# Second cross attention of a Perceiver-like kernel: maxima in two pieces, softmax by PSUM bank, and output products alternating with turned banks

## The chip, the cores and the metric

One core of one Trainium2 chip. The metric is the device time of one execution in microseconds (us), given as the median of several runs. TensorE does matrix products and transposes, VectorE and ScalarE elementwise work and reductions, GpSimd issues the gathers here, and SyncE issues the weight loads. All five run their own instruction streams and wait for each other by semaphores. PSUM, into which TensorE writes, has 8 banks of 512 fp32 columns; SBUF holds the rest.

## The reference, cut to what matters

Two layers, each of cross attention, self attention and a feed-forward part, on x of shape (2, 128, 512) with a context of (2, 2048, 512). The change is in the second layer's cross attention alone:

```python
def _L1_xattn_ref(q, kv, Wq, Wkv, Wc):            # q: layernorm(x), kv: the context
    qp = jnp.einsum('bld,ed->ble', q, Wq)
    scores = jnp.einsum('bld,bmd->blm', qp, kv)   # 128 x 2048 for each batch
    idx = jnp.argmax(scores, axis=-1)
    mem = jnp.take_along_axis(kv, idx[..., None], axis=1)   # 128 chosen rows
    mk, mv = jnp.split(jnp.einsum('bld,ed->ble', mem, Wkv), 2, axis=-1)   # 32 wide each
    qh = qp.reshape(b, l, 16, 32).transpose(0, 2, 1, 3)
    logits = jnp.einsum('bhld,bmd->bhlm', qh, mk) / sqrt(32)
    attn = softmax(logits)                        # 16 heads, 128 x 128 each
    out = jnp.einsum('bhlm,bmd->bhld', attn, mv)  # then heads side by side
    return jnp.einsum('bld,ed->ble', out, Wc)     # added to x
```

## The kernel before

Each part of the model is one function per engine (`..._pe`, `..._act`, `..._dve` for TensorE, ScalarE and VectorE), and the order in each function is written by hand; no scheduler changes it. The parts follow one another on every engine: first cross attention, mixer, experts, then `cross1_*` (the part in question), `linear_*` and the feed-forward part. A part starts with a norm of x_res: statistics on VectorE, a square root on ScalarE, and eight transposes on TensorE. While TensorE waits, `keep_clock(pe, bank, n)` lets it do n products of no use (an identity by constants, 256 columns) into a spare bank. A fp32 product is two records in the trace, a transpose one.

Weights come as 151 blocks of 1 MB through a ring of four, issued by SyncE; a block's slot is loaded again when `blk_used` says that it was read. The stage uses two of them (`BLK_X1` for the queries, `BLK_X1 + 1` for the output). The context comes back into SBUF by GpSimd's queue (`ctx_back`), during the last expert and the start of the stage.

The stage before, with the batches b = 0 and 1:

1. TensorE: queries `qpT` (L1817), copied by ScalarE (L1886). Then the scores of batch 0 in banks 4 to 7 and of batch 1 in banks 0 to 3, 16 products of 512 columns each (L1827).
2. VectorE, for each batch: the eight largest of 2048 columns (L1907), their index (L1909), and the row's number `pick` (L1911). GpSimd gathers the chosen rows by an indirect DMA into `mem` (L2306).
3. TensorE turns `mem` (L1836) for each batch, with 16 fillers between the two; ScalarE copies it to `memT` (L1889). Keys of both batches in one go (L1840), then values of both (L1844).
4. VectorE spreads the keys by heads into `mkz` (L1914), ScalarE copies the values (L1891). TensorE makes the logits of one batch in four banks (L1853), four heads a bank.
5. VectorE: maximum over each head (L1919) and subtraction (L1920) of a whole batch, 128 x 2048. ScalarE: the exponential of the whole batch (L1894). VectorE: sum (L1923), reciprocal (L1924) and scaling (L1925) of the whole batch. TensorE has 15 fillers meanwhile.
6. TensorE turns the 16 heads of a batch (L1862), ScalarE copies each bank (L1897), TensorE mixes the values with weights of 32 columns (L1867), ScalarE copies the result (L1900), and TensorE makes the output product in banks 2 and 3 (L1875), all for batch 0 and then batch 1.
7. VectorE adds both batches' output to x_res in one operation (L1927), from which the next norm starts.

Of the kernel before, what the change touches and what calls it, by code (L numbers as in the profile page):

```python
# [16 lines left out]
P = 128  # L17
# [98 lines left out]
def build(nc, x, ctxT, ctx_rows, wq, wk, wv, wo, stream, small, cols, rows, consts, out):  # L116
# [6 lines left out]
    with ExitStack() as ctx:  # L123
# [3 lines left out]
        def sem(name):  # L127
            return ctx.enter_context(nc.semaphore(name))
# [153 lines left out]
        NORM_WAIT = {1: (12, 2), 2: (7, 3), 3: (7, 2), 4: (7, 5)}  # L282
# [1500 lines left out]
        top8 = [sb(f"top8_{b}", [P, 8]) for b in range(B)]  # L1783
        at8 = [sb(f"at8_{b}", [P, 8], u32) for b in range(B)]
        pick = [sb(f"pick{b}", [P, 1], u32) for b in range(B)]
        lm = sb("lm", [P, B, H])
        ls = sb("ls", [P, B, H])

        ctx_back = [sem(f"ctx_back{b}") for b in range(B)]
        qp_filled = sem("qp_filled")  # L1790
# [8 lines left out]
        mk_filled = sem("mk_filled")  # L1799
        mkz_ready = sem("mkz_ready")  # L1800
        mv_filled = sem("mv_filled")
        mv_ready = sem("mv_ready")
        la_filled = sem("la_filled")
        la_shift = sem("la_shift")
# [5 lines left out]
        x1o_ready = sem("x1o_ready")  # L1810

        def cross1_pe(pe):
            norm_pe(pe, 3)
            need(pe, BLK_X1)
            for ec in range(C):
# [4 lines left out]
                if ec % 2:  # L1820
                    last.then_inc(qp_filled if ec == 1 else blk_used, 1)
            pe.wait_ge(qp_ready, 2)
            for b in range(B):
                pe.wait_ge(ctx_back[b], KB * 16)
                for kb in range(KB):
                    for c in range(C):
                        last = nc.tensor.matmul(psum[:, 4 - 4 * b + kb, :], qpT[:, c, b * P:(b + 1) * P],  # L1827
                                                ctxT_sb[b][kb][:, c, :], start=c == 0, stop=c == C - 1)
                last.then_inc(pick_scores, 1)
            pe.wait_ge(at_found, 1)  # L1830
            for b in range(B):
                if b:
                    keep_clock(pe, 7, 16)
                pe.wait_ge(mem_arrived[b], 16)
                for c in range(C):
                    last = nc.tensor.transpose(psum[:, 4 + b, c * P:(c + 1) * P], mem[:, b, c * P:(c + 1) * P], C_("ident"))  # L1836
                last.then_inc(memT_filled, 1)
            pe.wait_ge(memT_ready, 2)
            for c in range(C):
                last = nc.tensor.matmul(psum[:, 6, 0:T], S_("x1_k")[:, c, :], memT[:, c, :], start=c == 0, stop=c == C - 1)  # L1840
            last.then_inc(mk_filled, 1)
            for b in range(B):
                for c in range(C):
                    last = nc.tensor.matmul(psum[:, 7, b * DK:(b + 1) * DK], memT[:, c, b * P:(b + 1) * P],  # L1844
                                            S_("x1_v")[:, c, :], start=c == 0, stop=c == C - 1)
            last.then_inc(mv_filled, 1)
            pe.wait_ge(at_found, 2)
            for b in range(B):
                pe.wait_ge(mkz_ready, b + 1)
                if b == 1:  # L1850
                    pe.wait_ge(mv_ready, 1)
                for j in range(C):
                    last = nc.tensor.matmul(psum[:, 4 * b + j, :], qpT[:, j, b * P:(b + 1) * P], mkz[:, b, :, :],  # L1853
                                            start=True, stop=True)
                last.then_inc(la_filled, 1)
            pe.wait_ge(la_shift, 1)
            keep_clock(pe, 3, 15)
            for b in range(B):
                pe.wait_ge(la_ready, b + 1)
                for j in range(C):  # L1860
                    for i in range(4):
                        last = nc.tensor.transpose(psum[:, 4 * b + j, i * P:(i + 1) * P], la[:, b, 4 * j + i, :], C_("ident"))  # L1862
                    last.then_inc(laT_filled, 1)
            for b in range(B):
# [543 lines left out]
```

## Time and profile before

| | us |
|---|---|
| median of 3 runs | 1406.88 |
| the 3 runs | 1405.14, 1406.88, 1409.73 |
| the profiled execution | 1404.22 |
| its span, first to last instruction | 1402.4 |
| mean granted TensorE clock | 0.974 of full |

In the chain that ended last each piece is an engine at work, or "issue" where nothing shown held it back. In the timeline a row is a merged run of instructions with its start, its length and the idle time before it in brackets. The windows view gives for each stretch the busy time of each engine and the clock that TensorE was granted (1.00 is 2.4 GHz, 0.50 is 1.2 GHz; a number between is a mean over both).

### The profile page before, as it was taken

Reading aid. Unit: us, or ns where it says so; the run is one execution under the profiler, and the core shown is the slowest. Engines: PE = TensorE matmul, PEld = TensorE weight load, DVE = VectorE, ACT = ScalarE, POOL = GpSimd, SP = SyncE. Lnnn points to the kernel's source line nnn. Section 1 sums busy time; section 2 is a strip of 40 time slices with the busy share of each in tenths; the row PEclk is TensorE's granted clock in tenths of the full one; section 3 lists DMA queues with packets and bytes.
Section 4 is the critical chain, followed back from the end, with each engine's and each line's share of the span. In section 5 each row is a group of like instructions: output and inputs, shape, how many; then the busy total and the mean of one; then the engine's idle time right before and its main releaser. Section 6 shows DMA issues by size and latency. Waiting matters only on the chain.

```text
span 1402.4 us, 23487 instructions
## 1 busy us (share of the span) xinstructions
PE 1329.9 (95%) x9866; PEld 1136.3 (81%) x9866; DVE 904.0 (64%) x1131; ACT 679.1 (48%) x754; POOL 12.0 (1%) x18
## 2 busy tenths in 40 slices
PE   7999999999999999896899999999898889999998
PEld 6899999889999986665577777777655669999997
DVE  4665666766566656697778888888425667444443
ACT  4534444544444442652377777777303144555442
POOL 0000000000000000000000000000100000000000
PEclk9999999999999999895899999999999999999999
DMA  8111011401010030120089899999920315455552
GB/s 284 35 31 35 20 42 50 124 20 35 20 35 20 20 121 21 71 80 13 30 318 343 344 341 336 341 344 357 348 90 0 120 64 189 172 183 188 186 185 79
DMA packets 50219, 197.66 MB, mean 141 GB/s; under 512 B 12112, under 2 KB 20560, under 8 KB 30416
## 3 DMA queue, kind: packets, MB, share of 16 engines
q1 hardware_dynamic: 47792, 187.41, 36.8%
q0 software_dynamic: 2336, 8.91, 1.8%
q8 instruction: 72, 1.18, 0.3%
q14 instruction: 19, 0.16, 0.0%
HBM read 195.78 MB, written 0.52 MB: 140 GB/s over the span
## 4 chain that ended last, share of the span: by engine, by line
PE 85%; DVE 10%; issue 2%; ACT 1%; DMA 1%; SPq 0%; POOL 0%; POOLq 0%; DVEq 0%; ACTq 0%
PE psum L453 13%; PE psum L2128 13%; PE psum L428 13%; PE psum L1538 8%; PE psum L480 5%; PE psum L1558 4%; PE psum L1541 4%; PE psum L505 4%; PE psum L2110 3%; PE psum L1561 2%; PE psum L2141 2%; PE psum L1570 1%; PE psum L1958 1%; PE psum L464 1%; PE psum L1827 1%
## 5 line engine op out<-in xcount | busy, mean ns | idle before, releaser
L1599 DVE TENSOR_TENSOR arena_r<-ring,arena_r 128x2048 fp32r<-128x2048 f32 x96 | 219.7, 2290 | 35.7 <-ACT arena_r L1593 35.4
L453 PE MATMUL psum<-ring_r,arena_r 128*128 128x256 f32 x1536 | 201.4, 290 | 3.5 <-ACT arena_r L723 2.5
L453 PEld LDWEIGHTS psum<-ring_r,arena_r 128*128 128x128 f32 x1536 | 192.1, 194 | 4.2 <-issue 2.7
L428 PE MATMUL psum<-arena_r 128*128 128x512 f32 x768 | 186.0, 398 | 9.3 <-ACT arena_r L757 9.2
L1593 ACT CAST arena_r<-ring 128x2048 fp32r<-128x2048 f32 x96 | 183.5, 1913 | 16.5 <-PE psum L1541 10.8
L2128 PE MATMUL psum<-arena_r 128*128 128x256 f32 x1536 | 184.5, 283 | 1.1 <-DVE arena_r L2187 1.1
L2128 PEld LDWEIGHTS psum<-arena_r 128*128 128x128 f32 x1536 | 184.4, 192 | 1.2 <-issue 1.2
L428 PEld LDWEIGHTS psum<-arena_r 128*128 128x128 f32 x768 | 143.1, 190 | 41.6 <-issue 8.4
L2081 DVE TENSOR_TENSOR arena_r<-ring,arena_r 128x2048 fp32r<-128x2048 f32 x44 | 100.9, 2292 | 117.0 <-ACT arena_r L2076 117.0
L2076 ACT CAST arena_r<-ring 128x2048 fp32r<-128x2048 f32 x44 | 83.8, 1904 | 111.4 <-PE psum L2128 85.2
L1538 PE MATMUL psum<-arena_r 128*128 128x512 f32 x512 | 132.5, 401 | 1.3 <-issue 1.3
L1538 PEld LDWEIGHTS psum<-arena_r 128*128 128x128 f32 x512 | 94.2, 188 | 23.2 <-issue 5.0
L744 ACT COPY arena<-psum 128x1024 f32<-128x1024 f32 x64 | 61.7, 1016 | 89.6 <-PE psum L480 89.6
L616 DVE TENSOR_TENSOR arena<-arena,psum 128x1024 f32<-128x1024 f32 x64 | 75.2, 1216 | 28.0 <-PE psum L494 28.0
L301 DVE TENSOR_TENSOR arena_r<-arena,arena_r 128x768 fp32r<-128x768 f32 (+2 forms) x25 | 33.8, 1354 | 74.4 <-ACT arena_r L715 56.2
L736 ACT COPY ring<-psum 128x512 f32<-128x512 f32 x64 | 37.2, 582 | 87.1 <-PE psum L453 87.1
L751 ACT ACTIVATE arena<-arena 128x1024 f32<-128x1024 f32 x64 | 66.2, 1058 | 19.8 <-DVE arena L616 18.5
L596 DVE TENSOR_TENSOR arena<-arena 128x512 f32<-128x512 f32 (+1 forms) x128 | 71.5, 559 | 4.4
L1541 PE MATMUL psum<-arena_r 128*128 128x512 f32 x256 | 68.7, 390 | 0.0
L480 PEld LDWEIGHTS psum<-qT,arena 64*128 64x128 f32 x1024 | 59.7, 188 | 9.9 <-issue 9.1
L480 PE MATMUL psum<-qT,arena 64*128 64x128 f32 x1024 | 65.8, 278 | 0.8 <-issue 0.8
L1558 PE MATMUL psum<-arena_r 128*128 128x512 f32 x256 | 64.2, 393 | 0.0
(309 smaller groups left out, 1692.5 us busy)
## 6 DMA issues: line engine op xcount, KB each, us to landing
ring<-in_stream SPq DMA_DIRECT2D x151, 1024.0 KB, 4.9
arena<-in_ctxT POOLq DMA_DIRECT2D x8, 1024.0 KB, 12.3
arena<-in_ctxT SPq DMA_DIRECT2D x7, 1024.0 KB, 7.9
arena<-in_wk SPq DMA_DIRECT2D x16, 256.0 KB, 3.3
wv_in<-in_wv SPq DMA_DIRECT2D x8, 512.0 KB, 3.4
arena<-in_wq SPq DMA_DIRECT2D x16, 256.0 KB, 2.5
arena<-in_wk SPq DMA_DIRECT2D x16, 128.0 KB, 3.2
arena<-in_wo SPq DMA_DIRECT2D x2, 1024.0 KB, 6.3
```

The lines of the kernel that those rows point to most:

```text
L428: last = nc.tensor.matmul(bank, wk_sb[wp][:, c, w], cx[xp][kb][:, c, :], start=c == wp == xp == 0, stop=c == C - 1 and xp == 1)
L453: last = nc.tensor.matmul(bank[:, q * T:(q + 1) * T], cx[xp][kc // 4][:, c, kc % 4 * P:(kc % 4 + 1) * P], wv_sb[wp][:, c, :], start=c == w ...
L480: last = nc.tensor.matmul(psum[:, 2 * half + kc // 4, kc % 4 * P:kc % 4 * P + P], kT[j % 2][a:a + 64, k0:k0 + P], qT[a:a + 64, j % 2, half ...
L616: nc.vector.tensor_tensor(part, part, per_row(psum[:, SPREAD_BANK, 0:P], KC // 2), ALU.subtract).then_inc(shifted, 1)
L1538: nc.tensor.matmul(out, xg[xp][:, c, e, :], hi[:, c, :], start=c == xp == 0, stop=False)
L1541: last = nc.tensor.matmul(out, xg[0][:, c, e, :], lo[:, c, :], start=False, stop=c == C - 1)
L1558: nc.tensor.matmul(psum[:, 5, :], hT[u][hp][:, f, :], hi[:, f, :], start=u == f == hp == 0, stop=False)
L1593: nc.scalar.copy(mwhi[p % MB], ring[k % RING][:, :]).then_inc(moe_hi, 1)
L1599: nc.vector.tensor_tensor(mwlo[p % MB], ring[(BLK_MOE + p) % RING][:, :], mwhi[p % MB].bitcast(fp32), ALU.subtract).then_inc(moe_lo if p < ...
L2076: nc.scalar.copy(whi[j % 2], ring[k % RING][:, :]).then_inc(w_hi, 1)
L2081: nc.vector.tensor_tensor(wlo[j % 2], ring[(BLK_W12 + j) % RING][:, :], whi[j % 2].bitcast(fp32), ALU.subtract).then_inc(w_lo, 1)
L2128: last = nc.tensor.matmul(psum[:, 4 + s, 0:T], w[wp][:, c, :], src[xp][:, c, :], start=c == wp == xp == 0, stop=c == FC - 1 and wp == 1)
```

## The change

Steps 2 to 7 are done by batch and by bank:

- The maximum of the scores is taken in two pieces, over the first 1536 and the last 512 columns, and a third small maximum joins them (`top16`).
- The turning of batch 0's rows and its keys and values stand between batch 1's score products, and batch 0's logits right behind them. The keys and values are made for one batch at a time. 7 fillers stand ahead of batch 1's rows; the 16 and the 15 of before are gone.
- Each bank of logits has its own maximum on VectorE, which is negated and scaled into `nlm`. ScalarE takes the exponential of each head from PSUM with `nlm` as bias, and gives the sum of the head as its accumulator output (`ls`). Subtraction and sum on VectorE are gone; reciprocal and scaling stay, by bank.
- The copies of batch 0's turned banks and of its mixed output move from ScalarE to VectorE; those of batch 1 stay on ScalarE, a bank at a time.
- The values are mixed by bank, 128 columns a product instead of 512. The output product of batch 0 is made in quarters between the turned banks of batch 1; batch 1's quarters follow as their copies arrive.
- x_res is added to in two halves, the first when batch 0's output is complete.
- The fillers of the norm behind the stage write bank 3 instead of 5.

The core of the diff, TensorE first:

```diff
+            def pick_part(b, parts):
+                for n in parts:
+                    kb, c = n // C, n % C
+                    last = nc.tensor.matmul(psum[:, PICK_BANK[b] + kb, :], qpT[:, c, b * P:(b + 1) * P],
+                                            ctxT_sb[b][kb][:, c, :], start=c == 0, stop=c == C - 1)
...
+            def turn_la(b, j):
+                pe.wait_ge(la_ready, C * b + j + 1)
+                for i in range(4):
+                    last = nc.tensor.transpose(psum[:, PICK_BANK[b] + j, i * P:(i + 1) * P], la[:, b, 4 * j + i, :], C_("ident"))
+                last.then_inc(laT_filled, 1)
+
+            def mix_mem(b, j, out):
+                pe.wait_ge(laT_ready, C * b + j + 1)
+                for i in range(4):
+                    last = nc.tensor.matmul(out[DK * i:DK * i + DK, :], mvt[:, b, :], laT[:, b, 4 * j + i, :], start=True, stop=True)
+                return last
...
+            pe.wait_ge(ctx_back[0], KB * 16)
+            pick_part(0, range(0, 12)).then_inc(pick_scores, 1)
+            pick_part(0, range(12, 16)).then_inc(pick_scores, 1)
+            pe.wait_ge(ctx_back[1], KB * 16)
+            pick_part(1, range(0, 8))
+            turn_mem(0)
+            pick_part(1, range(8, 10))
+            project_mem(0)
+            pick_part(1, range(10, 12)).then_inc(pick_scores, 1)
+            pick_part(1, range(12, 16)).then_inc(pick_scores, 1)
+            logits(0)
             pe.wait_ge(at_found, 2)
...
+            keep_clock(pe, 3, 7)
+            turn_mem(1)
+            project_mem(1)
+            logits(1)
+            for j in range(C):
+                turn_la(0, j)
+            for j in range(C):
+                last = mix_mem(0, j, psum[:, PICK_BANK[0], j * P:(j + 1) * P])
+            last.then_inc(x1o_filled, 1)
             need(pe, BLK_X1 + 1)
...
+            turn_la(1, 0)
+            pe.wait_ge(x1o_ready, 1)
+            out_x1(0, 0)
+            for j in range(1, C):
+                turn_la(1, j)
+                last = out_x1(0, j)
+                if j == C - 1:
+                    last.then_inc(x1_proj, 1)
+                mix_mem(1, j - 1, psum[:, PICK_BANK[1] + j - 1, 0:P]).then_inc(x1o_filled, 1)
+            pe.wait_ge(x1o_ready, 2)
+            out_x1(1, 0)
+            mix_mem(1, C - 1, psum[:, PICK_BANK[1] + C - 1, 0:P]).then_inc(x1o_filled, 1)
+            for c in range(1, C):
+                pe.wait_ge(x1o_ready, c + 2)
+                last = out_x1(1, c)
             last.then_inc(blk_used, 1)
...
+            def exp_la(b, j):
+                act.wait_ge(lm_ready, C * b + j + 1)
+                for i in range(4):
+                    h = 4 * j + i
+                    ins = nc.scalar.activation(la[:, b, h, :], psum[:, PICK_BANK[b] + j, i * P:(i + 1) * P], ACT.Exp,
+                                               bias=nlm[:, b, h:h + 1], scale=LA_SCALE, accum_out=ls[:, b, h:h + 1])
+                ins.then_inc(la_exp, 1)
...
+                dve.wait_ge(pick_scores, 2 * b + 1)
+                nc.vector.max(top16[b][:, 0:8], scores[:, 0:1536])
+                dve.wait_ge(pick_scores, 2 * b + 2)
+                link(dve, nc.vector.max(top16[b][:, 8:16], scores[:, 1536:]))
+                nc.vector.max(top8[b][:, :], top16[b][:, :]).then_inc(top_found, 1)
```

VectorE's order in `cross1_dve` decides when the banks move, and it is long, so it is shown as the instructions that it issues. TensorE's old order from the scores on, as rows taken away (the name `arena` holds all of the stage's tensors, `cst` the constants, `sml` the key and value weights, `ring` the weight blocks):

```order
-L1827 MATMUL psum<-arena 128x512 x32
-L1836 MATMUL psum<-cst,arena 128x128 x4
-L279 MATMUL psum<-cst 128x256 x16
-L1836 MATMUL psum<-cst,arena 128x128 x4
-L1840 MATMUL psum<-arena,sml 128x256 x4
-L1844 MATMUL psum<-sml,arena 128x32 x8
-L1853 MATMUL psum<-arena 128x512 x8
-L279 MATMUL psum<-cst 128x256 x15
-L1862 MATMUL psum<-cst,arena 128x128 x32
-L1867 MATMUL psum<-arena,mvt 32x512 x8
-L1875 MATMUL psum<-ring,arena 128x512 x8
```

The same place of the changed kernel up to batch 1's logits, where L1837 are scores, L1844 turned rows, L1850 and L1854 keys and values, and L1862 logits:

```order
+L1837 MATMUL psum<-arena 128x512 x24
+L1844 MATMUL psum<-cst,arena 128x128 x4
+L1837 MATMUL psum<-arena 128x512 x2
+L1850 MATMUL psum<-arena,sml 128x128 x4
+L1854 MATMUL psum<-sml,arena 128x32 x4
+L1837 MATMUL psum<-arena 128x512 x6
+L1862 MATMUL psum<-arena 128x512 x4
+L279 MATMUL psum<-cst 128x256 x7
+L1844 MATMUL psum<-cst,arena 128x128 x4
```

Batch 0's rows, keys and values moved from behind the scores to between them, and its logits in front of batch 1's rows.

TensorE of the changed kernel behind the logits of batch 1, where L1868 are turned banks, L1874 mixing and L1878 output quarters:

```order
+L1868 MATMUL psum<-cst,arena 128x128 x16
+L1874 MATMUL psum<-arena,mvt 32x128 x16
+L1868 MATMUL psum<-cst,arena 128x128 x4
+L1878 MATMUL psum<-ring,arena 128x512
+L1868 MATMUL psum<-cst,arena 128x128 x4
+L1878 MATMUL psum<-ring,arena 128x512
+L1874 MATMUL psum<-arena,mvt 32x128 x4
```

The last three rows come three times in all, less the first turn; then come batch 1's quarters with one mixing group among them. Before, all 32 turns, all mixing and all output products stood in three blocks.

VectorE behind the second index, before:

```order
-L1914 TENSOR_TENSOR arena<-psum,col 128x512 x2
-L1919 TENSOR_REDUCE lm<-psum 128x16
-L1920 TENSOR_TENSOR arena<-psum,lm 128x2048
-L1919 TENSOR_REDUCE lm<-psum 128x16
-L1920 TENSOR_TENSOR arena<-psum,lm 128x2048
-L1923 TENSOR_REDUCE ls<-arena 128x16
-L1924 RECIPROCAL ls<-ls 128x16
-L1925 TENSOR_TENSOR arena<-arena,ls 128x2048
```

And in the changed kernel, from batch 1's last two maxima to the end of its first scaling (L1995 and L1996 maximum and negation, L2001 and L2002 reciprocal and scaling, L2006 copies of batch 0's turned banks):

```order
+L1995 TENSOR_REDUCE lm<-psum 128x4
+L1996 TENSOR_SCALAR nlm<-lm 128x4
+L1995 TENSOR_REDUCE lm<-psum 128x4
+L1996 TENSOR_SCALAR nlm<-lm 128x4
+L2001 RECIPROCAL ls<-ls 128x4
+L2002 TENSOR_TENSOR arena<-arena,ls 128x512
+L2006 COPY arena<-psum 128x512 x4
+L2001 RECIPROCAL ls<-ls 128x4
+L2002 TENSOR_TENSOR arena<-arena,ls 128x512
```

Each operation has a quarter of its old columns, and the four copies that ScalarE had stand between the last scaling of batch 0 and the first of batch 1.

## Rows read from the trace of the kernel before

**Rows 1.** The page: busy time by engine, and the last chain's shares by engine.

```profile
PE 1329.9 (95%) x9866; PEld 1136.3 (81%) x9866; DVE 904.0 (64%) x1131; ACT 679.1 (48%) x754; POOL 12.0 (1%) x18
PE 85%; DVE 10%; issue 2%; ACT 1%; DMA 1%; SPq 0%; POOL 0%; POOLq 0%; DVEq 0%; ACTq 0%
```

**Rows 2.** The chain that ended last, in the stage: start us, length us, what.

```profile
1015.35 14.02 PE psum L1827 x32
1029.39 2.31 DVE top L1907
...
1048.29 3.44 DMA arena<-in_ctx_rows,pick
...
1055.10 1.70 PE psum L1844 x16
...
1060.36 2.30 DVE lm L1919
...
1062.68 2.29 DVE arena L1920
...
1069.49 2.20 DVE ls L1923
...
1072.01 2.29 DVE arena L1925
...
1076.82 2.30 DVE arena L1925
...
1079.16 1.97 PE psum L1862 x16
1081.13 1.90 PE psum L1867 x16
1083.03 7.08 PE psum L1875 x16
1090.13 1.23 DVE x_res L1927
```

**Rows 3.** Timeline of TensorE and VectorE in the stage.

```profile
1015.35 27.73 PE L1827 MATMUL psum<-arena 128*128 128x512 f32 x64 [0.67 <-ACT arena L1886]
...
1043.12 2.30 DVE L1907 MAX8 top<-psum 128x8 f32<-128x2048 f32 x1 [8.85 <-PE psum L1827]
...
1051.77 0.65 PE L1836 MATMUL psum<-cst,arena 128*128 128x128 f32 x4 [1.34 <-DMA arena<-in_ctx_rows,pick]
...
1089.93 3.19 PE L279 MATMUL psum<-cst 128*128 128x256 f32 x14
```

**Rows 4.** Groups by line and shape, and two timeline rows: operations like the added ones.

```profile
L261 DVE COPY xnT<-psum 128x512 f32<-128x512 f32 x5 | 3.5, 692 | 4.6 <-PE psum L290 4.6
L1667 DVE TENSOR_TENSOR gt_top<-gt_rank,grm 128x16 f32<-128x16 f32 x2 | 0.3, 175 | 0.1
L1889 ACT COPY arena<-psum 128x512 f32<-128x512 f32 x2 | 1.2, 586 | 36.6 <-PE psum L1836 36.6
L1189 ACT ACTIVATE arena<-cst,gdec 128x128 f32<-128x128 f32 x32 | 9.4, 386 | 0.0
L1177 ACT ACTIVATE alog<-row 128x16 f32<-128x16 f32 x1 | 0.2, 199 | 0.0
...
587.62 9.44 ACT L1189 ACTIVATE arena<-cst,gdec 128x128 f32<-128x128 f32 x32
657.49 3.71 PE L1127 MATMUL psum<-arena 128*32 128x128 f32 x64 [1.27 <-DVE arena L1280]
```

**Rows 5.** TensorE's idle time, and windows: length, busy times, granted clock, DMA.

```profile
1074.36 3.43 PE L1862 MATMUL psum<-cst,arena 128*128 128x128 f32 x16 [2.59 <-DVE arena L1925]
...
1074.00:1075.00 1.00, 0.64 (x4) 0.65 (x5) 1.00 (x2) 0.00 (x0) 0.00 (x0) 0.82 0.00 0
1075.00:1076.00 1.00, 1.00 (x7) 1.00 (x6) 1.00 (x1) 0.59 (x1) 0.00 (x0) 0.50 0.00 0
1078.00:1079.00 1.00, 0.00 (x0) 0.00 (x0) 1.00 (x1) 0.41 (x1) 0.00 (x0) 0.97 0.00 0
...
1122.00:1125.00 3.00, 2.64 (x3) 1.13 (x4) 2.90 (x8) 1.94 (x2) 0.00 (x0) 0.57 0.00 0
...
658.00:661.00 3.00, 3.00 (x61) 2.53 (x54) 1.96 (x2) 0.60 (x1) 0.00 (x0) 0.50 0.02 5
```

More of the change, by code:

```diff
@@ L1783, in build @@
         top8 = [sb(f"top8_{b}", [P, 8]) for b in range(B)]
+        top16 = [sb(f"top16_{b}", [P, 16]) for b in range(B)]
         at8 = [sb(f"at8_{b}", [P, 8], u32) for b in range(B)]
@@ L1820, in cross1_pe @@
                 if ec % 2:
-                    last.then_inc(qp_filled if ec == 1 else blk_used, 1)
+                    last.then_inc(x1_proj if ec == 1 else blk_used, 1)
             pe.wait_ge(qp_ready, 2)
[L1823 to L1833, printed above, removed]
+            def pick_part(b, parts):
[4 more added lines that the diff above has]
+                return last
+            def turn_mem(b):
@@ L1856, in cross1_pe @@
[L1856 to L1864, printed above, removed]
-                pe.wait_ge(laT_ready, C * (b + 1))
-                for i in range(4):
-                    last = nc.tensor.matmul(psum[DK * i:DK * i + DK, b, :], mvt[:, b, :],
-                                            laT[:, b, :, :].rearrange("p (j i) q -> p j i q", i=4)[:, :, i, :],
-                                            start=True, stop=True)
-                last.then_inc(x1o_filled, 1)
@@ L1886, in cross1_act, with copy_mem @@
                 nc.scalar.copy(qpT[:, 2 * i:2 * i + 2, :], psum[:, 2 + i, :].rearrange("p (c t) -> p c t", c=2)).then_inc(qp_ready, 1)
[L1887 removed]
+            def copy_mem(b):
                 act.wait_ge(memT_filled, b + 1)
[L1889 to L1891 removed]
@@ new lines, in cross1_act, with copy_laT, copy_x1o @@
+            copy_mem(0)
+            copy_mv(0)
+            exp_la(0, 0)
+            exp_la(0, 1)
+            copy_mem(1)
+            exp_la(0, 2)
+            copy_mv(1)
+            exp_la(0, 3)
+            for j in range(C):
+                exp_la(1, j)
+            def copy_laT(j):
+                act.wait_ge(laT_filled, C + j + 1)
+                nc.scalar.copy(laT[:, 1, 4 * j:4 * j + 4, :], bank4(PICK_BANK[1] + j)).then_inc(laT_ready, 1)
+            def copy_x1o(j):
+                act.wait_ge(x1o_filled, j + 2)
+                nc.scalar.copy(x1oT[:, j, P:T], psum[:, PICK_BANK[1] + j, 0:P]).then_inc(x1o_ready, 1)
@@ new lines, in cross1_dve @@
+            pick_dve(0)
+            spread_mk(0)
+            pick_dve(1)
+            for j in range(C):
+                largest_la(0, j)
+            scale_la(0, 0)
+            spread_mk(1)
+            scale_la(0, 1)
+            largest_la(1, 0)
+            largest_la(1, 1)
+            scale_la(0, 2)
+            largest_la(1, 2)
+            largest_la(1, 3)
+            scale_la(0, 3)
+            for j in range(C):
+                copy_laT(0, j)
+            scale_la(1, 0)
+            dve.wait_ge(x1o_filled, 1)
```

124 lines of the change are left out of this document (65 added, 59 removed).

## Prediction, made before the changed kernel was run

> **What bounds the kernel now.** I read the page first: TensorE is busy 95% of the span and carries 85% of the chain that ended last, VectorE 10% [rows 1]. Such an average says nothing of the second layer's cross attention, so I next read the chain through that stage, from the first row-choosing product at 1015.35 us to the sum into x_res at 1090.13 us [rows 2]. There the chain leaves TensorE: the two batches go through VectorE in whole-batch operations of 2.2 to 2.3 us, and each engine waits for the whole batch of the one before. From 1060.36 to 1079.12 the chain is VectorE alone: maximum, subtraction, sum, reciprocal and scaling of 16 x 128 numbers, for two batches [rows 2]. In the timeline of that stretch TensorE runs only fillers. So a gain here is a gain of the whole kernel, up to the point where the chain goes back to TensorE. Behind the stage everything starts from x_res, and its weight blocks are released by the same two counts as before, so I take the later stages as shifted and not changed.
>
> **The change, step by step.** All times are on the clock of the profiled execution; the old end of the stage is 1090.13 + 1.23 = 1091.35 us [rows 2].
>
> *To the second gather.* The scores of batch 0 end in two pieces (24 and 8 records). The maximum over the first 1536 columns runs under the last 8 records; behind them stand a maximum over 512 columns, at most 0.70 us by the 128x512 copy out of PSUM [rows 4], and one over 16 numbers, about 0.2 us by the smallest VectorE groups (0.17 us) [rows 4]. They take the place of one of 2.30 us [rows 3]: 1.4 us saved. From the start of that old maximum to the landing of the rows it was 1051.73 - 1043.12 = 8.61 us [rows 2, 3], now 7.2 us. Batch 0's rows then land at 1029.39 + 7.2 = 1036.6 us. TensorE has by then run 8 of batch 1's 16 products (0.43 us a record, 64 in 27.73 us [rows 3]), to 1036.0, and waits about 0.6 us. Turning the rows takes 4 x 0.107 = 0.43 us, and the keys and values of batch 0, 16 short records, about 1.7 us (16 in 1.70 us [rows 2]). These three, 2.8 us, now stand in front of the end of batch 1's scores, 1043.1 + 2.8 = 1045.9 us. Its maximum saves 1.4 us again, so the second rows land at 1053.1 instead of 1051.7 us: **1.4 us later**. In exchange the first batch's logits (8 records of 0.43) are done by 1049.1 us, while VectorE looks for the index. The filler there is 14 records, some 3.1 us by the 14 in 3.19 [rows 3]; it ends at 1052.4, before the rows land, and costs nothing. It would cost only if the gather landed more than 0.8 us earlier.
>
> *From the rows to batch 1's first logits.* Turn and drain 0.65 us [rows 3], ScalarE copy 0.59 [rows 4], keys and values 1.7, the values' copy about 0.3, first bank of logits 0.86 + 0.3 to drain: 1057.8 us. Before, the second batch's logits started only behind the first's. Meanwhile VectorE has taken batch 0's four maxima and scaled two banks.
>
> *The softmax by bank.* The subtraction goes away (it becomes ScalarE's bias) and the sum too (ScalarE's accumulator). Each was 2 x 2.3 us on VectorE [rows 2]. Left are, a bank, a maximum of 0.70 plus a tiny negation 0.17, and a reciprocal 0.17 plus a scaling 0.70. From 1057.8 VectorE has four maxima with negation and two scalings, 6 x 0.87 = 5.2 us, then four copies of turned banks, 2.8 us, the first scaling of batch 1, 0.87, and the copy of batch 0's output, 0.7: to 1067.4 us. The turned banks' copies must wait for the last scaling in VectorE's order, and TensorE's mixing waits for them; TensorE is mostly idle from 1061.3 to 1067. This VectorE stretch is what ends last.
>
> *ScalarE's price.* It now runs 32 exponentials of 128 columns with a bias from SBUF. The nearest row, 32 of 128x128 with a per-partition operand, took 9.44 us together, 0.295 apiece though one alone lasts 0.386 [rows 4]. No row shows an accumulator output. Below I take nothing for it (0.295 in all). Above, a second short instruction that does not overlap, 0.20 us like the 16-column one [rows 4], added to a lone 0.386: 0.59. I take 0.45, between the two, nearer the overlapped row. At 0.45 a bank costs 1.8 us and batch 1 is through at about 1065.9, just in time for the scalings that VectorE reaches at 1066; up to 0.45 the price is hidden, at 0.59 it adds 1.5 us.
> The Trainium skill, VectorE: DVE Perf Modes, section "Two Vector instructions with no wait between them", says of VectorE that an operation with an accumulator output is two instructions, the main one and a read. It is not said of ScalarE there, and no row of this case shows it for either; were it so here, the upper value would be the one to take.
>
> *The output quarters.* From 1067.4 TensorE has 16 records of 512 columns (8 products, 6.9 us), three turns (1.3 us) and four mixing groups, in one row with all waits met early. A mixing group is 8 records with 32 columns of weights: 64 such took 3.71 us at half clock [rows 4, 5], so 0.46 a group at half clock and about 0.25 at full. Sum 9.2 to 10.0 us, to 1076.6 or 1077.4, 0.3 to drain, and the sum of one half instead of both, 0.70 instead of 1.23: the stage ends at 1077.6 to 1078.5, in the middle **1078.0**. That is 13.3 us before 1091.35. It holds the four gains together: 18.8 us of VectorE alone are cut to 9.6, the mixing and half of the output products lie under or beside them (1.90 and 3.5 us of the old chain), 0.5 us in the last sum, less 1.4 us for the later gather and what TensorE's alternation adds.
>
> *The clock.* The fillers fall from 31 products to 7. In the old stage TensorE was idle for 2.59 us behind its fillers, and from about 1074.7 the granted clock was 0.50, that is 1.2 of 2.4 GHz; it was back at 1.00 from 1078 [rows 5]. In the next stage, with four records and a gap of 2 us, the same fall comes (0.57 over 1122 to 1125) [rows 5]. Between 1061.3 and 1067.4 the new order gives TensorE four turns' and mixings' worth of some 2 us in 6: a fall there is as likely as not. It would double what runs for one such stretch; where that lies over 1064 to 1069, working the order through with doubled records moves the end by 0.8 to 2 us. I charge **1.0 us**.
> The 16 transposes from 1074.36 us in the old stage, all TensorE had to do until the rise at 1078, did not keep the clock down [rows 5]. The Trainium skill, TensorE: Matmul & The Clock Gate, section "Part 4: PE-mode transpose", holds that transposes do not count as activity for the clock gate; the trace disagrees. By the skill the clock would stay low into the output quarters, which is the rival of that name below.
>
> The smaller edits cost nothing measurable: another PSUM bank for the norm's fillers, x_res of batch 0 added under batch 1's products, and a copy of values in two parts under other work.
>
> **Sum.** 13.3 - 1.0 = 12.3 us. Against the profiled execution (1404.22 us, of which 1402.4 are the span) that is 1391.9; against the median of the three runs, 1406.88, which lies 2.7 above it, 1394.6. The forecast is a median too; I put it near the second, at **1394.0**.
>
> **Rivals.**
> *The clock stays low through the output quarters.* If the turns and short mixings do not keep or bring back the clock, all from about 1064 to 1072 is at half: the eight output products are then partly doubled and the order ends at 1081 to 1083 instead of 1078. Gain 8.5 to 10 us: about 1397.5. For it: idle 2.59 us was enough once. Against: the rise behind transposes at 1078 [rows 5], and that the output quarters are themselves dense. Chance 0.16.
> *ScalarE becomes the bound.* If an exponential with its sum takes 0.8 us, ScalarE's 16 in batch 1 end at about 1072 and the order ends at 1086: gain 5.3 us, 1401.5. At 0.6 it is 1394.6 + 1.5 = 1396. Against it: the rows' 0.295 [rows 4], and nothing else queues on ScalarE there. Chance 0.12, most of it near 1397 to 1398.
> *Slower than before.* The clock falls in the thin stretch of the second gather (about 1050 to 1056, fillers reduced there) and is not given back. With every TensorE record from 1049 on at half rate, the order ends at 1096.5, 5.2 us behind the old end: 1412. It decides from the point where the clock stays at 0.50 through the logits of batch 1 as well as the outputs; low only from 1061 on gives 1089, still not slower. Against it: the old kernel was as thin around 1052 and kept its clock, and each fall shown was taken back within some 4 us. Chance 0.02.
> *It does not do what it says*: VectorE's order (copies of turned banks behind the last scaling) cancels most of the overlap, for instance by waits that I hold as met. Gain under 4 us, about 1404. Chance 0.04.
> *Better than reckoned*: no fall of the clock, and mixing at its lower price: gain 13.7 us and more, 1392 or less. Chance 0.16. The forecast proper, gain 11 to 13.7, keeps 0.50.
>
> **How the numbers follow.** The range goes from a gain of 14.5 us on the profiled execution (1389.7) to one of 7 us on the median (1399.9): 1389.5 to 1400. It leaves out the last two rivals, and the far end of ScalarE's: under 0.15. A measurement of this kernel can tell about 0.3% (4.2 us) from no change. Faster by more than that holds the forecast, the better case, the clock and nearly all of ScalarE's: 0.94; within it 0.04; slower 0.02.
>
> **What the new profile would show.** Right: second gather landing about 1.4 us later on the same clock, no subtraction and no sum on VectorE, x_res complete 12 to 13 us earlier after the stage's first product, TensorE idle 4 us in pieces before the alternation and then dense for 9 to 10 us. Wrong: VectorE idle with ScalarE's exponentials as its releaser in batch 1 (the accumulator's price); granted clock 0.50 under the output products (the clock); output products waiting for ScalarE's copies (the alternation's waits are not met).

## The result, and the profile after

| | before | changed |
|---|---|---|
| median, 4 runs each | 1407.35 us | 1389.16 us |
| lowest to highest | 1405.14 to 1409.73 | 1386.37 to 1391.61 |
| ratio, 95% interval | | 0.9881 (0.9855 to 0.9907) |
| profiled execution, its span | 1404.22, 1402.4 | 1391.61, 1389.8 |

The change makes the kernel faster, by 16.7 us by the ratio (13.1 to 20.4). The two profiled spans differ by 12.6 us only. Where the rest may lie is the first question of the experiments.

I use one measure throughout: **the stage**, from the start of the first score product to the start of the statistics on x_res behind it. Before it is 76.04 us: from 1015.35 us [rows 2] to the statistics behind the sum, in the same chain:

```profile
1091.39 1.30 DVE stats L244 x2
```

In the changed kernel's first profile it is 63.55 us. Ahead of it the two profiles differ by 0.11 us, behind it both have 311.0 us left. The chain through the changed stage (start us, length us, what):

```profile
1015.24 14.01 PE psum L1837 x32
...
1029.28 0.71 DVE top L1980
...
1049.62 3.24 DMA arena<-in_ctx_rows,pick
...
1056.57 1.11 PE psum L1862 x2
...
1057.70 0.70 DVE lm L1995
...
1061.98 0.69 DVE arena L2002
1062.67 2.40 DVE arena L2006 x4
1065.06 0.10 DVE ls L2001
...
1065.18 0.70 DVE arena L2002
...
1066.02 1.08 PE psum L1868 x4
1067.11 1.48 PE psum L1878 x2
...
1069.88 0.36 PE psum L1874 x8
...
1075.25 2.79 PE psum L1878 x6
...
1078.06 0.70 DVE x_res L2032
...
1078.79 1.30 DVE stats L244 x2
```

The 2.3 us pieces of [rows 2] are gone but for the search of the index. VectorE is alone on the chain from 1057.70 to 1065.88 us, 8.2 us instead of 18.8, and from 1066.02 to 1078 the chain is TensorE without a gap. The second gather lands 37.62 us after the first score product, against 36.38 before, 1.2 us later.

The granted clock in this execution (length, busy times of PE, PEld, DVE, ACT and POOL, then the clock):

```profile
1062.00:1063.00 1.00, 0.28 (x2) 0.28 (x3) 1.00 (x2) 1.00 (x7) 0.00 (x0) 1.00 0.00 0
1065.00:1066.00 1.00, 0.65 (x8) 0.21 (x9) 0.97 (x4) 0.00 (x0) 0.00 (x0) 0.50 0.00 0
1067.00:1068.00 1.00, 1.00 (x3) 0.47 (x3) 0.97 (x3) 0.58 (x1) 0.00 (x0) 0.50 0.03 8
1069.00:1070.00 1.00, 1.00 (x11) 0.21 (x9) 0.00 (x0) 0.58 (x1) 0.00 (x0) 1.00 0.08 16
```

It fell to 0.50 (1.2 of 2.4 GHz) behind the thin stretch and came back at about 1068: the first turned bank took 1.08 us and the first output product 1.48 us of the chain.

### The profile page after: what moved, and what is told of

It is laid out like the page before. It is cut to its first block, busy times and chain, and to the rows that moved or that the text cites. A ratio compares the mean times of both kernels' runs of the same rounds, so it can differ in the third digit from the quotient of the medians.

```text
span 1389.8 us, 23595 instructions
## 1 busy us (share of the span) xinstructions
PE 1319.1 (95%) x9874; PEld 1127.0 (81%) x9874; DVE 901.5 (65%) x1163; ACT 684.6 (49%) x815; POOL 12.0 (1%) x18
## 4 chain that ended last, share of the span: by engine, by line
PE 84%; DVE 10%; issue 3%; ACT 2%; DMA 1%; SPq 0%; POOL 0%; POOLq 0%; DVEq 0%; ACTq 0%
PE psum L453 13%; PE psum L2233 13%; PE psum L428 13%; PE psum L1538 8%; PE psum L480 5%; PE psum L1558 4%; PE psum L505 4%; PE psum L1541 4%; PE psum L2215 3%; PE psum L1561 2%; PE psum L2246 2%; PE psum L2063 1%; PE psum L464 1%; PE psum L1570 1%; PE psum L1837 1%
```

## The experiments

All of them side by side; the text below takes them one by one. Times of whole executions scatter by some 10 us in a kernel, and the profiles show one place where: the first score product starts between 1011.0 and 1017.1 us, once at 1022.5, in kernels with the same code up to there. So the parts are told apart by the stage, each from one profile.

| kernel | stage us | clock at half rate in the stage | ratio to before (95%) |
|---|---|---|---|
| before, first profile | 76.04 | 1074.6 to 1078.0, ahead of a wait for VectorE | |
| before, again | 79.07 | 1049.3 to 1052.8 and 1076.6 to 1080.0 | 1.0009 (0.9972 to 1.0047) |
| changed, first profile | 63.55 | 1064.8 to 1068.2 | 0.9881 (0.9855 to 0.9907) |
| changed, again | 62.71 | none | 0.9898 (0.9866 to 0.9930) |
| before, softmax by bank | 69.50 | 1053.8 to 1057.3 | 0.9945 (0.9923 to 0.9967) |
| before, maxima in two pieces | 74.48 | 1068.9 to 1072.3, ahead of a wait for VectorE | 0.9980 (0.9959 to 1.0002) |
| changed, maxima in one piece | 65.51 | none | 0.9910 (0.9879 to 0.9942) |
| changed, outputs in blocks | 63.28 | none | 0.9875 (0.9847 to 0.9904) |
| changed, sums on VectorE | 66.96 | 1067.4 to 1074.2 | 0.9931 (0.9906 to 0.9956) |
| changed, exponentials twice | 66.62 | 1056.0 to 1062.9 | 0.9914 (0.9883 to 0.9946) |
| changed, no fillers | 66.51 | 1061.0 to 1071.3 | 0.9917 (0.9892 to 0.9942) |
| changed, 14 fillers | 64.98 | none | 0.9885 (0.9848 to 0.9921) |
| changed, filler in the thin stretch | 62.66 | none | 0.9880 (0.9855 to 0.9904) |
| that, and a copy on ScalarE | 62.20 | none | 0.9889 (0.9857 to 0.9922) |

### Where do the missing 4 us lie?

**Changed, again.** No edit.

> The changed kernel once more, unchanged. Call the stage the time from the first score product to the end of the last sum into x_res: 76.0 us before, 63.5 us in the first profile of the changed kernel. Theory: all of the gain is in the stage, and the rest of the program is the same to 0.2 us, so the stage is 63.5 us again (up to 1 us less if the clock does not fall in it) and the times lie 12.5 us under before, a ratio of 0.991. Rival: the timed runs of the first comparison (ratio 0.988, 16.7 us) show some 4 us more that the profile does not hold; then the ratio is 0.987 to 0.9885 again.

The stage was 62.71 us, with the clock at 1.00 all through it; the ratio 0.9898 lies between the two theories and excludes neither. The same order of instructions as in the first profile took 0.84 us less. The chain, with the place where the clock had been low in the middle:

```profile
1011.99 14.02 PE psum L1837 x32
...
1054.55 0.70 DVE lm L1995
...
1062.86 0.63 PE psum L1868 x4
1063.49 1.01 PE psum L1878 x2
...
1074.70 1.30 DVE stats L244 x2
```

The two in the middle are 1.08 and 1.48 us in the first profile: 0.9 us is the price of that fall. Every ratio of a kernel lies below what its stage gives against 76.04 us, by 0.6 to 5.1 us (outputs in blocks: 76.04 - 63.28 = 12.8 us is 0.991, measured 0.9875). What they share is the kernel before, so that was looked at again.

**Before, again.** No edit.

> The kernel before once more, unchanged, for a second profile of it. The ratios of the timed runs lie 0.0004 to 0.0036 below what the stages of the profiles give (about 3 us in the mean for kernels built from the changed one). Theory: in other executions of the kernel before, the clock falls at places of the stage where it costs something (under the output products, or the logits), so that its stage is 77 us or more; in the one profile so far the fall lay under a wait. Rival: the stage is 76.0 us again, and the few us lie in the part ahead of the stage, whose length varied from 1011 to 1022 us between profiles of kernels that have the same code there.

The theory held for the stage: it is 79.07 us, 3.03 us longer than in the first profile of the same kernel. The chain at the two falls:

```profile
1048.69 3.18 PE psum L1840 x8
1051.87 2.19 PE psum L1844 x16
...
1076.42 3.51 PE psum L1862 x16
```

In the first profile the second and the third took 1.70 and 1.97 us [rows 2], and the first 1.99:

```profile
1053.10 1.99 PE psum L1840 x8
```

Together that is 3.2 us more. One fall stands behind the wait for the second gather, one behind the wait for VectorE. In the first profile the clock fell as well, but its slow stretch lay under batch 0's transposes, with VectorE still to be waited for [rows 5], and cost nothing. So the profile from which I predicted showed the better of two stages of the kernel before. From 79.07 to 62.71 it is 16.4 us, from 76.04 to 63.55 it is 12.5: the timed 16.7 (13.1 to 20.4) and 14.3 us (9.8 to 18.8) lie in and around that.

Whether the longer old stage is what the timed runs hold beyond the first pair of profiles is not shown by this. Two profiles of the old kernel don't give how often each case happens. The execution with the long stage was not a long one: it took 1403.04 us, where the median of its 8 runs is 1407.22. And the interval of the second comparison (9.8 to 18.8) holds 12.5 us as well.

### What the parts are worth

**Before, with the softmax by bank alone.**

```diff
-                link(dve, nc.vector.reduce_max(lm[:, b, :], logits, AX.X))
-                nc.vector.tensor_tensor(la[:, b, :, :], logits, per_elem(lm[:, b, :], P), ALU.subtract).then_inc(la_shift, 1)
+                link(dve, nc.vector.reduce_max(lm[:, b, heads], bank4(n), AX.X))
+                nc.vector.tensor_scalar(nlm[:, b, heads], lm[:, b, heads], -LA_SCALE, None, ALU.mult).then_inc(la_shift, 1)
...
-                link(dve, nc.vector.reduce_sum(ls[:, b, :], la[:, b, :, :], AX.X))
...
-            keep_clock(pe, 3, 15)
+            keep_clock(pe, 3, 4)
```

> The kernel before with the softmax by bank alone: maximum, negated, as bias of ScalarE's exponentials from PSUM with their sums as accumulator output, reciprocal and scaling by bank, 4 fillers instead of 15; all else in the old order. Theory: VectorE's 18.8 us become 16 operations of 0.8 us from the first bank of logits at 1057.8 on, the last bank is scaled at about 1071 and the stage ends 9 us earlier: 67 us (66 to 68.5 with the clock). Rival: the order is what matters, the softmax only lets other waits come forth (ScalarE's copies, the blocks of turns), and the stage loses 5 us or less: 71 us or more.

The stage was 69.50 us, 1.0 us over the theory's range and better than the rival. The clock fell there, in code that this edit leaves alone. The chain:

```profile
1053.44 3.44 PE psum L1842 x8
1056.88 1.94 PE psum L1846 x16
...
1060.73 11.29 ACT arena L1897 x64
1072.02 3.90 ACT arena L1902 x8
```

The first two took 1.99 us and 1.70 us [rows 2] in the first profile of the kernel before: that is 1.7 us. Without it the stage would be 67.8 us, 0.8 over the 67 of the theory. Like for like, the softmax by bank is worth 76.04 - 67.8 = 8.2 us of the old kernel.

The path is not that of the theory. Not VectorE but ScalarE ends last here: 32 exponentials with their accumulator reads, back to back, and behind them the copies of all eight turned banks, 15.2 us together. The changed kernel has four of these copies on VectorE, and starts batch 0's exponentials before batch 1's rows are there. So the 8.2 us are the softmax by bank in the old order, where ScalarE holds it back.

**Before, with the maxima in two pieces alone.**

```diff
-                nc.vector.max(top8[b][:, :], scores).then_inc(top_found, 1)
+                nc.vector.max(top16[b][:, 0:8], scores[:, 0:1536])
+                dve.wait_ge(pick_scores, 2 * b + 2)
+                link(dve, nc.vector.max(top16[b][:, 8:16], scores[:, 1536:]))
+                nc.vector.max(top8[b][:, :], top16[b][:, :]).then_inc(top_found, 1)
```

> The kernel before with the maximum of the scores in two pieces alone. Theory: the index of each batch is found 1.4 us earlier, the second gather ends 1.4 us earlier and the chain runs through it; TensorE's 16 fillers end 0.1 us after that, so the stage is 1.3 us shorter: 74.7 us. Rival: the fillers or the first batch's rows hold TensorE anyway: 76.0 us.

74.48 us, 1.56 less than before, where the theory had 1.3. The time alone does not tell this kernel from the one before (0.9959 to 1.0002). The rows now land before TensorE is through with its 16 fillers, so the chain goes through the fillers:

```profile
1039.52 6.91 PE psum L279 x32
1046.43 0.45 PE psum L1838 x4
```

**Changed, with the maxima in one piece.** The edit is the reverse of the one above.

> The changed kernel with each maximum over 2048 columns in one piece. Theory: batch 0's rows come 1.4 us later and TensorE waits 1.8 instead of 0.4 us for them in the middle of batch 1's scores; batch 1's index comes 1.4 us later on top of that, and 0.4 us of TensorE's idle time behind the fillers does not absorb it: the second gather lands 2.8 us later. Batch 0's softmax is further on by then, so the end moves by 2 to 2.8 us: stage 65.5 to 66.3 us. Rival: the cost is only one piece, 1.4 us, as in the old order: 64.9 us.

65.51 us, 2.80 more than the 62.71 of the changed kernel at the same clock: the two maxima count twice here, because TensorE waits for batch 0's rows in the middle of batch 1's scores. The second gather lands 40.51 us after the first score product, against 37.71 in that profile. TensorE's wait for batch 0's rows in the timeline was 1.76 us, against 0.35:

```profile
1034.42 0.66 PE L1844 MATMUL psum<-cst,arena 128*128 128x128 f32 x4 [1.76 <-DMA arena<-in_ctx_rows,pick]
```

**Changed, with the outputs in blocks.**

```diff
-            turn_la(1, 0)
-            pe.wait_ge(x1o_ready, 1)
-            out_x1(0, 0)
-            for j in range(1, C):
-                turn_la(1, j)
-                last = out_x1(0, j)
...
+            for j in range(C):
+                turn_la(1, j)
+            for j in range(C):
+                mix_mem(1, j, psum[:, PICK_BANK[1] + j, 0:P]).then_inc(x1o_filled, 1)
+            pe.wait_ge(x1o_ready, 1)
+            for j in range(C):
+                last = out_x1(0, j)
```

> The changed kernel without the alternation: all four turned banks of batch 1, then its four mixings, then the eight output quarters; ScalarE's copies in the same order. Theory: the alternation only fills the waits for VectorE's last scalings and for ScalarE's copies, worth 0.6 to 1.5 us: stage 64.1 to 65.0 us. Rival: it is what the change is named for and carries more than 3 us of the gain: 66.5 us or more.

63.28 us, under the theory's range and the rival's. The alternation is worth 0.57 us against 62.71, and nothing that a time can tell. TensorE of that run:

```profile
1066.57 0.66 PE L1868 MATMUL psum<-cst,arena 128*128 128x128 f32 x4 [0.69 <-DVE arena L1995]
1067.38 0.66 PE L1868 MATMUL psum<-cst,arena 128*128 128x128 f32 x4 [0.16 <-DVE arena L1995]
1068.19 0.66 PE L1868 MATMUL psum<-cst,arena 128*128 128x128 f32 x4 [0.16 <-DVE arena L1995]
1068.78 1.17 PE L1874 MATMUL psum<-arena,mvt 128*32 128x128 f32 x32
1069.88 7.13 PE L1878 MATMUL psum<-ring,arena 128*128 128x512 f32 x16
```

In blocks TensorE waits 1.0 us for VectorE's last scalings, but the four mixings together take 1.17 us instead of 4 x 0.36 on the chain, and the output products have no transposes or short products between them. What the alternation fills it partly pays back.

### The prices and the rivals

**Changed, with the sums on VectorE.**

```diff
-                                               bias=nlm[:, b, h:h + 1], scale=LA_SCALE, accum_out=ls[:, b, h:h + 1])
+                                               bias=nlm[:, b, h:h + 1], scale=LA_SCALE)
...
+                link(dve, nc.vector.reduce_sum(ls[:, b, heads], la[:, b, heads, :], AX.X))
                 link(dve, nc.vector.reciprocal(ls[:, b, heads], ls[:, b, heads]))
```

> The changed kernel with the sum of each head on VectorE instead of ScalarE's accumulator output: eight reductions of 128x512 more on VectorE, 0.7 us each, 32 accumulator reads of 0.2 us less on ScalarE. Theory: VectorE ends last from the first logits of batch 1 on, and four of the eight stand on that stretch before the first output quarter: with the clock's fall hidden in part the stage is 1.7 to 2.8 us longer, 65.2 to 66.3 us. Rival: ScalarE is what ends last there, and freeing it pays for VectorE's work: 63.5 us or less.

66.96 us. The direction and the engine are those of the theory, the size is over it. Between batch 1's first logits and the first output quarter three sums of 0.60 us stand on the chain, and three reciprocals at 0.19 instead of 0.09: 2.1 us. The rest is the clock, which fell at 1067.4 us, behind a wait for VectorE that is now 2.47 us long, and stayed at half until 1074.2: the first two turned banks of batch 1 and the first two output quarters took 5.0 us on the chain instead of 2.9. The wait in the timeline, and a window in the slow stretch:

```profile
1065.64 0.66 PE L1868 MATMUL psum<-cst,arena 128*128 128x128 f32 x4 [2.47 <-DVE arena L2003]
```

```profile
1070.00:1074.00 4.00, 4.00 (x12) 2.24 (x10) 3.81 (x9) 1.17 (x2) 0.00 (x0) 0.50 0.00 0
```

**Changed, with each exponential twice.**

```diff
+                    nc.scalar.activation(laT[:, b, h, :], psum[:, PICK_BANK[b] + j, i * P:(i + 1) * P], ACT.Exp,
+                                         bias=nlm[:, b, h:h + 1], scale=LA_SCALE)
```

> The changed kernel with a second, useless exponential of each head on ScalarE, into a place that is overwritten later. An exponential with its accumulator read took 0.342 us a head in the profile; this makes it some 0.6 to 0.64. Theory: ScalarE has little slack in batch 1 (it is through at 1064.0, and the scaling that needs its fourth bank starts at 1068.1, but the second batch-0 scalings wait as soon as a bank costs more than 1.8 us): the prediction gave 1.5 us for 0.59 a head; here 1.5 to 4 us more, stage 65 to 67.5 us. Rival: ScalarE is far from the end and the doubling is hidden: 63.5 us.

66.62 us, inside the theory's range, by another way. A head costs 0.61 us now. ScalarE is late not in batch 1, but with the copy of batch 1's rows, which stands in its order behind eight exponentials of batch 0; TensorE waits 2.07 us for it instead of 0.68. The clock then fell on values and logits, and the rest of the 3.9 us over 62.71 lies there; this run does not tell what the doubled exponentials would cost without that fall. The chain there:

```profile
1054.22 0.35 ACT arena L1943 x2
1054.57 0.48 ACT arena L1931
...
1056.34 1.57 PE psum L1854 x8
...
1058.26 3.77 PE psum L1862 x4
```

**Changed, without the seven fillers.**

```diff
-            keep_clock(pe, 3, 7)
```

> The changed kernel without the seven fillers ahead of the second batch's rows. Theory: they hide behind the gather (TensorE still waits 0.4 us after them), so without them nothing moves directly; TensorE is idle for 3.7 us instead and the clock falls for one stretch around the keys, values and logits of batch 1. These are on the chain, so 1 to 2 us are lost: stage 64.5 to 65.5 us. Rival of that name in the prediction (the clock falls there and is not given back): 70 us or more. If the clock does not fall: 63.5 us.

66.51 us: 3.8 us over 62.71, more than the theory's 1 to 2 and less than the rival's 6.5. The gather lands at the same 37.62 us after the first score product, so the fillers are hidden, as said. But TensorE is idle for 3.78 us before the rows, and the clock is at half for 10.2 us, through keys, values and all logits of batch 1, as the timeline has it:

```profile
1060.21 0.63 PE L1844 MATMUL psum<-cst,arena 128*128 128x128 f32 x4 [3.78 <-DMA arena<-in_ctx_rows,pick]
1061.51 2.08 PE L1850 MATMUL psum<-arena,sml 128*128 128x128 f32 x8 [0.68 <-ACT arena L1930]
...
1065.50 6.54 PE L1862 MATMUL psum<-arena 128*128 128x512 f32 x8 [0.37 <-ACT mvt L1934]
```

It came back, as in every fall seen; only later than I had taken from the two falls before.

**Changed, with 14 fillers.** `keep_clock(pe, 3, 14)` instead of 7.

> The changed kernel with 14 instead of 7 fillers ahead of the second batch's rows. Theory: the seven end 0.4 us before the rows land, so seven more (3.1 us) push the rows' transposes by 2.7 us; VectorE and ScalarE have all of batch 0's softmax done by then, which gives back under 1 us: stage 65.4 to 66.2 us. Rival: batch 1's rows are not on the chain and the stage is 63.5 us.

64.98 us, 2.3 over 62.71 and 0.4 under the range, which stood on the stage of 63.5; as an increment it is within the theory's 1.9 to 2.7. TensorE goes from the last filler to the rows without a wait, where it waited 0.40 us for them behind seven. Seven fillers fit the wait to within that.

**Changed, with fillers in the thin stretch.**

```diff
             for j in range(C):
+                if j == C - 1:
+                    pe.wait_ge(la_exp, C + 1)
+                    keep_clock(pe, PICK_BANK[1], 4)
                 turn_la(0, j)
```

> The changed kernel with four fillers (about 1.8 us of TensorE) in a free bank, between the third and the fourth turned bank of batch 0, where TensorE waits 1.2 us for VectorE. Theory: the granted clock fell to 0.50 from 1064.9 to 1068.2 us because TensorE did little from 1061.6 on; with the fillers it stays at 1.00 there, the first turned bank of batch 1 and the first output quarter take 0.5 and 0.9 us instead of 1.0 and 1.7, and the stage ends 1.1 us earlier: 62.4 us. Rival: the clock falls all the same (then 63.5), or the fillers push the fourth turned bank past VectorE's copy of it and the stage is 63.5 or longer.

62.66 us at clock 1.00, near the 62.4 of the theory. It proves little: the unedited kernel at clock 1.00 had 62.71. What it shows is that 1.8 us of TensorE there cost nothing. Whether they prevent the fall that came in one of two profiles of the unedited kernel stays open.

**That, with one of VectorE's copies on ScalarE** (three fillers).

```diff
-            for j in range(C):
+            for j in range(C - 1):
                 copy_laT(0, j)
...
+            act.wait_ge(laT_filled, C)
+            nc.scalar.copy(laT[:, 0, 4 * C - 4:4 * C, :], bank4(PICK_BANK[0] + C - 1)).then_inc(laT_last, 1)
```

> The changed kernel with ScalarE instead of VectorE copying the fourth turned bank of batch 0, and three fillers as in the run with fillers. Theory: VectorE alone ends last from 1057.7 to 1066.5 us; one copy less there brings the first output quarter forward by 0.5 us, on top of the clock: 61.9 us, the fastest of all. Rival: ScalarE is through with the exponentials only at 1064.0 and its copy comes as late as VectorE's did: 62.4 us.

62.20 us, the shortest stage, 0.5 us under the run before, which has four copies on VectorE and one filler more. On the chain VectorE's copies before the first scaling of batch 1 are three:

```profile
1058.42 1.80 DVE arena L2015 x3
1060.22 0.10 DVE ls L2010
```

By its stage it beats both kernels; in time it can't be told from the changed one (0.9889 and 0.9881).

## Why the prediction was right, and where it was not

The forecast was 1394.0 us, faster. Measured were 1389.16 us, 0.3 us under the low end of the range. By the ratio, 0.9881, on the median that the forecast started from (1406.88) it is 1390.1 us, just inside. The direction, the stage and the path were as predicted; the gain was larger than the forecast's 12.9 us.

- **The sum of the schedule: right in total, in part by luck.** I worked out 13.3 us without the clock, and the stages at no cost of the clock are 76.04 and 62.71: 13.3 us. From the start of the stage to VectorE's first maximum of batch 1 it took 42.56 us in the changed kernel's second profile, worked out 42.45. From there to the first output quarter it was 8.9 us, worked out 9.6; from there to the statistics 11.2, worked out some 10.6. Two errors of 0.6 to 0.7 us with opposite signs cancelled. That VectorE ends last up to batch 1's first scaling and TensorE from there on, held.
- **The second gather** landed 1.2 us later, worked out 1.4.
- **From the rows to the first logits.** The terms that I listed add up to 4.4 us and not to the 4.7 that I used. It took 4.85 us in the second profile: keys and values of one batch are 1.16 and 0.83 us, where I had taken the 1.70 of a row that holds values alone. The slip in adding happened to cover that.
- **ScalarE's price.** I took 0.45 us a head between 0.295 and 0.59; it is 0.342. The timeline of the changed kernel has a separate read of the accumulator behind each exponential, which overlaps with it:

```profile
1058.63 0.37 ACT L1941 ACTIVATE arena<-psum,nlm 128x128 f32<-128x128 f32 x1 [0.80 <-DVE nlm L1996]
1058.90 0.19 ACT L1941 ACTIVATION_READ_ACCUMULATOR arena<-psum,nlm 128x1 f32 x1
1058.99 0.36 ACT L1941 ACTIVATE arena<-psum,nlm 128x128 f32<-128x128 f32 x1
```

  The Trainium skill says, in VectorE: DVE Perf Modes, section "Two Vector instructions with no wait between them", that an operation with an accumulator output is two instructions. It says so of VectorE; the trace shows the same for ScalarE. The second one adds 0.05 us to the 0.295 of [rows 4], not its length.
- **VectorE's operations** were each 0.07 to 0.09 us cheaper than I took them when they followed one another, 2.40 us for four copies of 0.69. The stretch took 8.2 us to the first scaling of batch 1, worked out 8.9.
- **The output stretch** was longer than worked out. The 16 records of the output products held 7.4 us of the chain in the second profile (worked out 6.9) and the three turned banks among them 1.6 (1.3). The mixing is 0.36 us a group at full clock, where I had estimated 0.25 for full and 0.46 for half; four groups are 1.4 us, inside the 1.0 to 1.8 of the sum.
- **The clock.** For the new stage I charged 1.0 us. The fall that I described did come, in the stretch that I named, and cost 0.84 us in the first profile; in the second it did not come. What I had wrong is the other side of the comparison: I let the clock cost the old stage nothing, because in that one profile its fall was hidden [rows 5]. The same old kernel loses 3.0 us to the clock in another execution. So from one execution to another the clock can add to the gain instead of taking 1.0 us off. Whether that is why the timed gains, 16.7 and 14.3 us, lie above the forecast is not shown.
- **The base.** I saw that the profiled execution lay 2.7 us under the median. Its stage was the shorter one of two profiled; whether that is a part of the 2.7 us stays open.
- **The rivals.** The measured time is that of "better than reckoned" (1392 us or less, chance 0.16), but only one of its conditions was met, and in one profile of two: no fall of the clock. The mixing was not at its lower price. The clock staying low through the output quarters did not happen in the changed kernel; with the sums on VectorE it happened in half (at half rate until 1074.2). At 0.342 us ScalarE did not become the bound in the changed kernel, but it was the bound with the softmax by bank in the old order; at 0.61 us it held up the changed kernel by the copy of batch 1's rows, and not by the exponentials of batch 1. For the slower side I wrote that each fall was taken back within some 4 us; without the fillers it was 10.2 us. That cost 3.8 us, where the rival, with the clock at half to the end of the stage, had 18.
- **The signs.** TensorE was idle for 2.2 us in pieces between its first turned bank and batch 1's, not 4. From the first output quarter on it was dense for 10.5 us in the second profile, where I had 9 to 10.
- **Transposes and the clock.** I weighed what the Trainium skill says (TensorE: Matmul & The Clock Gate, "Part 4: PE-mode transpose": transposes don't count as activity) against one rise behind transposes. There are three by now. In the second profile of the old kernel 16 transposes are all that TensorE ran from 1076.42 to 1079.93 us, with the clock at half from 1076.6, and 0.1 us later it was back at 1.00. In the run with the maxima in two pieces the clock fell at 1068.9 and rose again at 1072.3 us, while TensorE was still in its 16 transposes and had run nothing else since 1068.79:

```profile
1068.79 3.63 PE L1864 MATMUL psum<-cst,arena 128*128 128x128 f32 x16 [2.59 <-DVE arena L1930]
```

  The trace disagrees with the Trainium skill each time.

What each part gives, like for like: softmax by bank 8.2 us in the old order, maxima in two pieces 1.6 (2.8 in the new order), the alternation 0.6, the last sum in halves 0.5 (1.23 and 0.70 us in the two chains). That leaves 2.4 us, or 1.2 with the 2.8. It is a remainder and not a measurement, and nothing here tells its parts apart: batch 0's rows, keys and logits under the scores, its turning under batch 1's softmax, and four of ScalarE's copies on VectorE. No run has the new order of the batches without the softmax by bank.

## What to carry to other kernels

One profile gives one execution's clock: where TensorE has waits (falls came behind 1.1 to 3.8 us of them here), take the same stage from a second profile before a gain is set against it, since a fall can be hidden in one and cost 3 us in the next. Where the chain runs through whole-batch operations of one engine, cutting them to what a PSUM bank holds and moving a pass into another engine's instruction (a bias, an accumulator output) gave 8.2 of 13.3 us, and left the chain on the engine that took the work over until the order and the copies were changed too; the finer alternation on TensorE gave 0.6 us. Compare parts by the length of their stage in profiles when whole times scatter by more than the part is worth.

## What the runs showed of the hardware that I had not expected

- The clock at half rate lasted 3.4 us in most falls within the stage, 6.8 us in two (sums on VectorE, exponentials twice) and 10.2 us in one (no fillers), with TensorE at work for most of each; ahead of the last, TensorE had been idle for 3.78 us. Two profiles of one kernel had their falls at different places or, for the changed one, in one of the two only.
- The accumulator read of ScalarE is an instruction of 0.19 to 0.29 us that costs 0.05 us behind an exponential of 128 columns (0.342 instead of 0.295 us a head).
- The last product of the self attention behind the stage is slower in some executions as well: in three of the profiles 312.8 us instead of 311.0 remained behind the stage, its four records taking 3.78 us instead of 1.98, at a granted clock of 0.50. In the timeline of the changed kernel's second profile:

```profile
1112.98 3.78 PE L2070 MATMUL psum<-ring,arena 128*128 128x512 f32 x4 [0.69 <-DVE arena L2131]
```
